# Score range from sums and absolute differences of key pairs, with key differences formed ahead of the loop

## The chip, the cores and the metric

The kernel runs on one core of one Trainium2 chip. A core has TensorE (PE; its weight loads are shown apart as PEld), VectorE (DVE), ScalarE (ACT), GpSimd (POOL) and SyncE (SP), which here only issues transfers. The metric is the device time of one execution in microseconds (us). Before the change the median of three runs is 1267.35 us (1264.89 to 1267.72).

## The reference, cut to what matters

32 samples of 153 rows (25 image rows, 128 text rows), 192 channels. Embedding, then attention with 12 heads of 16 channels in emulated integer arithmetic, then a layer of three experts. The change touches one step of attention, the range of all scores:

```python
attn = jnp.einsum('bhnd,bhmd->bhnm', q, k) * attn_scale
attn, a_scale = fq_act(attn)          # needs attn.min() and attn.max() over everything
attn = log_int_softmax(attn, a_scale) # needs the maximum of each row
```

`fq_act` takes its scale from the smallest and the largest score of all samples, heads and rows. So nothing of the softmax can begin until all scores have been formed once. The kernel forms them twice: once for the range and the row maxima (`range_scores`), and again in `attention`.

## The kernel before, in words

The program is a row of stages, each a block that ends for all engines together: `embed`, `quant_inputs`, `range_h`, `quant_qkv`, `range_scores`, `attention`, `project`, `ffn_inputs`, `experts`. Quantized queries and keys lie in `qk` (bf16) with four heads in the four partition groups of 32, three such tiles of queries and three of keys for each sample.

`range_scores` loops over the 32 samples ("batches", B), two by two, so that each engine has two buffers (`u` is 0 or 1). For one batch there are RT = 15 rows of score tiles: 12 heads with the 128 text queries, and 3 tiles in which the image queries of four heads are stacked. Each tile is 128 x 153.

To keep the heads of one tile apart, a head's keys (or image queries) are copied into a buffer that is zero in the other partition groups: `kb` for keys, `qb` for image queries. The class `Stage` holds this. `load` (lines 677 to 683), on SyncE, issues four transfers for `kb`, one for each partition group, and four more for `qb` if `placing` is false. If `placing` is true, as in `range_scores`, GpSimd writes `qb` with four copies (`place`, line 685). `attention` uses the same class with `placing` false. `free` (line 672) lets a load begin when TensorE has finished the batch two before it. The helper `wait_apart` (line 320) is a wait and, as an instruction of its own, a step of a semaphore `passed`.

Around it, in `range_scores` (line 712 on): TensorE makes five banks of three tiles (L708), each as soon as ScalarE has emptied the same bank of the last batch. ScalarE copies each bank to `score_copy` (L769); before the first bank of a batch it waits until VectorE is done with the copy two before. VectorE takes each row's maximum into `rmax` (L808) and, in a second pass over the same 2295 elements, the smallest value of all (L809). After the loop come small chained steps on VectorE (L814 to L855) for the range and its constants, one reduction over partitions on GpSimd, and on ScalarE, after its last bank, copies into `vbd` (L777) and `pick` (L779). SyncE, after its last load, fills `kb` and `qb` for the first two batches of `attention` when TensorE is done with them.

At the stage's start GpSimd clears `qb` and half of `kb` (L740, L741) and VectorE the other half (L798); SyncE's first transfer waits for all three.

Of the kernel before, what the change touches and what calls it, by code (L numbers as in the profile page):

```python
# [16 lines left out]
P = 128  # L17
# [30 lines left out]
def ds(start, size):  # L48
    return bass.ds(start, size)
# [21 lines left out]
def embed(k, m):  # L71
# [6 lines left out]
    with ExitStack() as st:  # L78
# [17 lines left out]
        img_acc, img_out, conv_ok = k.sem("img_acc"), k.sem("img_out"), k.sem("conv_ok")  # L96
        feat_set, feat_sq, feat_ok, featT_ps, featT_sb, emb_acc = (k.sem(x) for x in ("feat_set", "feat_sq", "feat_ok", "featT_ps", "featT_sb", "emb_acc"))
        power_set, stats1, aggr1, var1_ok, rstd1_ok, scaled_ok, h_ok = (
            k.sem(x) for x in ("power_set", "stats1", "aggr1", "var1_ok", "rstd1_ok", "scaled_ok", "h_ok"))
# [9 lines left out]
        with nc.Block() as block:  # L109
# [14 lines left out]
            @block.gpsimd  # L124
            def _(pool):
                pool.wait_ge(in_ids, 16)

                def gather(g):
                    for b in range(4 * g, 4 * g + 4):
                        pool.indirect_dma_start(out=raw[:, b, :], out_offset=None, in_=d["turns"],  # L130
                                                in_offset=bass.IndirectOffsetOnAxis(ap=ids[:, b:b + 1], axis=0)
                                                ).then_inc(gathered[g % 4], 16)

                def root1(g):
                    pool.wait_ge(aggr1, 4 * g + 4)
# [12 lines left out]
                pool.wait_ge(power_set, 1)  # L148
# [100 lines left out]
            def _(v):  # L249
                v.memset(feat[:, :, :], 0.0).then_inc(feat_set, 1)  # L250
                v.wait_ge(feat_set, 1)
                v.memset(feat[:, :, 0:8], 1.0).then_inc(feat_set, 1)
                v.memset(power[:, :, :], -0.5).then_inc(power_set, 1)
                v.memset(m["vt"][:, :, :], 0.0)
                v.memset(m["vi"][:, :, :], 0.0)
                v.wait_ge(feat_set, 2)

                def features(g):
                    rows = slice(4 * g, 4 * g + 4)
# [41 lines left out]

                features(0)
                v.wait_ge(in_conv, 32)
                v.tensor_tensor(convb[:, :], convb[:, :], posimg[:, :], ALU.add).then_inc(conv_ok, 1)
                v.wait_ge(conv_ok, 1)
                for g in range(G):
                    if g + 1 < G:
                        features(g + 1)
# [352 lines left out]
class Stage:  # L661

    def __init__(self, k, m, name, placing):

        self.m, self.placing = m, placing
        self.kb, self.qb = m["kb"], m["qb"]
        self.loaded = [k.sem(f"{name}_loaded{i}") for i in range(2)]
        self.placed, self.scored = k.sem(name + "_placed"), k.sem(name + "_scored")  # L670
# [41 lines left out]
def range_scores(k, m):  # L712


    NB = RT // 3
    with ExitStack() as st:
        sb = lambda n, s, t=F32: k.sb(n, s, t, st)
        s = Stage(k, m, "rs", True)
        low, copy, spent = sb("score_low", [P, B]), sb("score_copy", [P, 2, RT, N]), sb("score_spent", [P, 2, RT * N], BF16)
        rmax, con, ident, pick = m["rmax"], m["con"], m["ident"], m["pick"]  # L720
        mm1, mm2, own = sb("sm1", [P, 2]), sb("sm2", [P, 2]), sb("pick_own", [P, RT])
        banks = k.ps("rs_banks", [P, NB, 512], F32, st)
        cleared, kept, topped, lowered, sr, sred, vbd_zero = (
            k.sem(x) for x in ("rs_cleared", "rs_kept", "rs_topped", "rs_lowered", "rs_r", "rs_red", "vbd_zero"))
        vbd, own_ok = m["vbd"], k.sem("pick_own_ok")

        def pairs(eng, body):
# [9 lines left out]
        with k.nc.Block() as block:  # L737
            @block.gpsimd
            def _(pool):
                pool.memset(m["qb"][:, :, :, :, :], 0.0).then_inc(cleared, 1)  # L740
                pool.memset(m["kb"][:, 1, :, :, :], 0.0).then_inc(cleared, 1)  # L741
                pool.wait_ge(cleared, 3)
                pairs(pool, lambda n, u: s.place(pool, n, u))
                pool.wait_ge(sr, 1)
                pool.partition_all_reduce(mm2[:, :], mm1[:, :], P, RMAX).then_inc(sred, 1)

            @block.sync
            def _(sp):
                sp.wait_ge(cleared, 3)
                s.load(sp, 0, 0)  # L750
                s.load(sp, 1, 1)
                with sp.Fori(1, B // 2) as i:
                    for u in range(2):
                        s.load(sp, i * 2 + u, u)

                for u in range(2):
                    sp.wait_ge(s.scored, (B - 1 + u) * NB)
                    m["at_stage"].load(sp, u, u)

            @block.scalar  # L760
            def _(act):
                def body(n, u):
                    for b in range(NB):
                        act.wait_ge(s.scored, n * NB + b + 1)
                        if b == 0 and not early(n, 2):

                            act.wait_ge(topped, n - 1)
                            act.wait_ge(lowered, n - 1)
                        act.activation(copy[:, u, 3 * b:3 * b + 3, :].rearrange("p w n -> p (w n)"), banks[:, b, 0:3 * N], ACT.Copy).then_inc(kept, 1)  # L769
                pairs(act, body)  # L770

                act.wait_ge(vbd_zero, 1)
# [7 lines left out]

            @block.tensor
            def _(pe):
                def body(n, half, u):
                    s.ready(pe, n, half, u)
                    for b in range(NB):
                        if not early(n, 1):
                            pe.wait_ge(kept, (n - 1) * NB + b + 1)
                        s.scores_at(pe, n, u, b, banks[:, b, :])
# [7 lines left out]
            def _(v):  # L796
# [7 lines left out]
                with v.Fori(0, B // 2) as i:  # L804
                    for u in range(2):
                        n = i * 2 + u
                        v.wait_ge(kept, n * NB + NB)
                        v.tensor_reduce(rmax[:, n, :], copy[:, u, :, :], AX, ALU.max).then_inc(topped, 1)  # L808
                        v.tensor_scalar(spent[:, u, :], copy[:, u, :, :].rearrange("p t n -> p (t n)"), 1.0, BIG, ALU.mult, ALU.min,  # L809
                                        accum_out=low[:, ds(n, 1)]).then_inc(lowered, 1)  # L810
                v.wait_ge(topped, B)
                v.wait_ge(lowered, B)
                flat = lambda x: x[:, :, :].rearrange("p b t -> p (b t)")
                link(v.tensor_reduce(mm1[:, 0:1], flat(rmax), AX, ALU.max))  # L814
                link(v.tensor_reduce(mm1[:, 1:2], low[:, :], AX, ALU.min, negate=True))
# [4 lines left out]
                v.tensor_scalar(mm1[:, :], mm1[:, :], con[:, 0:1], None, ALU.mult).then_inc(sr, 1)  # L820
                v.wait_ge(sred, 1)
                quant_params(v, link, mm2, qa)
                inv = qa[:, 1:2]
# [20 lines left out]
                link(v.tensor_scalar(flat(rmax), flat(rmax), c(0), None, ALU.mult))  # L844
# [862 lines left out]
def build(nc, d):  # L1707
    with ExitStack() as stack:
# [25 lines left out]
        with att:  # L1734
# [8 lines left out]
            m["at_stage"] = Stage(k, m, "at", False)  # L1743
            range_scores(k, m)
            attention(k, m)
            project(k, m)
# [69 lines left out]
```

## Time and profile before

| what | value |
|---|---|
| median of three runs | 1267.35 us |
| the profiled execution's own time | 1267.97 us |
| its span, first to last instruction | 1266.2 us |
| mean granted TensorE clock | 0.73 |
| VectorE busy | 1081.3 us, 85% |
| ScalarE busy | 716.5 us, 57% |
| TensorE busy | 701.3 us, 55% |
| GpSimd busy | 92.1 us, 7% |
| key blocks loaded by SyncE (both stages) | 256 transfers of 28.7 KB |

Busy time is the time in which an engine works on an instruction; issuing transfers, register and semaphore instructions are not counted in it. "Idle before, releaser" is the time for which an engine stood still ahead of an instruction, and what ended it. SPq is SyncE's queue: the start and the length of the instruction that issues a transfer, not of the transfer. "To landing" is the time from an issue to the transfer's completion. The clock is a share of TensorE's full 2.4 GHz; 0.50 is its other level, 1.2 GHz. Matmul records overlap, so a group's mean length is longer than the distance between two.

### The profile page before, as it was taken

Reading aid. Unit: us, or ns where it says so; the run is one execution under the profiler, and the core shown is the slowest. Engines: PE = TensorE matmul, PEld = TensorE weight load, DVE = VectorE, ACT = ScalarE, POOL = GpSimd, SP = SyncE. Lnnn points to the kernel's source line nnn. Section 1 sums busy time; section 2 is a strip of 40 time slices with the busy share of each in tenths; the row PEclk is TensorE's granted clock in tenths of the full one; section 3 lists DMA queues with packets and bytes.
Section 4 is the critical chain, followed back from the end, with each engine's and each line's share of the span. In section 5 each row is a group of like instructions: output and inputs, shape, how many; then the busy total and the mean of one; then the engine's idle time right before and its main releaser. Section 6 shows DMA issues by size and latency. Waiting matters only on the chain. (4 is left out here: it accounts for less than half of the span.)

```text
span 1266.2 us, 22220 instructions
## 1 busy us (share of the span) xinstructions
PE 701.3 (55%) x5608; PEld 486.4 (38%) x5609; DVE 1081.3 (85%) x2534; ACT 716.5 (57%) x1271; POOL 92.1 (7%) x203
## 2 busy tenths in 40 slices
PE   4850165744544346657665666656423031299997
PEld 3640144433322123334333333334212021288987
DVE  5768898879999979999999999999999657566676
ACT  0451000955445559999999999999921221144543
POOL 5830000012121000000000000000000000000000
PEclk9875576975555576787878877877757555599999
DMA  4001000001111110101001000010000300245543
GB/s 147 3 1 62 0 0 0 1 7 30 24 23 25 20 34 20 24 22 22 20 19 24 22 21 19 22 23 17 10 1 1 140 0 0 102 147 195 189 175 110
DMA packets 84216, 54.48 MB, mean 43 GB/s; under 512 B 53688, under 2 KB 83160, under 8 KB 83928
## 3 DMA queue, kind: packets, MB, share of 16 engines
q1 hardware_dynamic: 83160, 53.97, 13.9%
q0 software_dynamic: 1024, 0.13, 0.2%
q8 instruction: 14, 0.23, 0.1%
q14 instruction: 18, 0.15, 0.0%
HBM read 11.77 MB, written 3.76 MB: 12 GB/s over the span
## 5 line engine op out<-in xcount | busy, mean ns | idle before, releaser
L1166 DVE SCALAR_TENSOR_TENSOR expo<-expo,con,pow 128x153 f32<-128x153 f32 x480 | 146.1, 375 | 0.7 <-ACT expo L1118 0.7
L769 ACT ACTIVATE score_copy<-rs_banks 128x459 f32<-128x459 f32 x160 | 74.7, 564 | 92.5 <-DVE score_spent L809 74.8
L1013 PE MATMUL at_pT<-identb,vi 128*128 128x128 bf16 x480 | 61.1, 292 | 90.4 <-ACT vi L1092 89.9
L1118 ACT ACTIVATE expo<-at_rem,con 128x459 f32<-128x459 f32 x160 | 97.0, 642 | 15.8 <-PE at_rem L998 8.3
L708 PE MATMUL rs_banks<-kb,qk 128*128 128x153 bf16 x384 | 57.7, 329 | 84.7 <-ACT score_copy L769 72.3
L997 PE MATMUL at_rem<-below,identb 128*128 128x459 bf16 x160 | 69.1, 432 | 60.3 <-ACT expo L1118 58.9
L603 ACT ACTIVATE qi<-pq,biasp,ap 128x306 int16<-128x306 f32 x96 | 48.0, 727 | 94.0 <-PE pq L566 94.0
L1215 DVE CUSTOM_DVE_ANT_0 weight_top<-weight_top,line 128x2448 uint16<-128x2448 uint16 x64 | 83.8, 1351 | 8.5 <-ACT line L1109 5.7
L1081 ACT ACTIVATE octave<-at_banks,con 128x459 int16<-128x459 f32 x160 | 90.2, 650 | 0.8 <-PE at_banks L708 0.2
L703 PE MATMUL at_banks<-pick,row_top 128*128 128x459 bf16 x160 | 78.2, 489 | 17.7 <-ACT octave L1081 17.1
L808 DVE TENSOR_REDUCE rmax<-score_copy 128x2295 f32 x32 | 81.3, 2542 | 4.1 <-ACT score_copy L769 4.1
L1191 DVE TENSOR_TENSOR expo<-expo,inv_total 128x1224 f32<-128x1224 f32 x64 | 83.6, 1347 | 0.0
L1013 PEld LDWEIGHTS at_pT<-identb,vi 128*128 128x128 bf16 x480 | 42.3, 129 | 104.6 <-issue 76.4
L809 DVE TENSOR_SCALAR_CACHE_REDUCE score_spent<-score_copy 128x2295 bf16<-128x2295 f32 x32 | 81.2, 2536 | 0.0
L1610 PE MATMUL e_p<-X,e_ws 128*128 (+1 forms) x960 | 72.2, 235 | 13.4 <-DMA e_ws<-w1l 13.2
L1109 ACT ACTIVATE line<-expo,p_index 128x1224 f32<-128x1224 f32 x64 | 76.6, 1251 | 2.0 <-DVE expo L1191 2.0
L708 PEld LDWEIGHTS rs_banks<-kb,qk 128*128 (+1 forms) x384 | 35.8, 126 | 104.2 <-issue 81.0
L1649 ACT ACTIVATE e_g<-e_p,b1s 128x153 f32<-128x153 f32 x192 | 58.9, 392 | 29.4 <-PE e_p L1610 28.2
L1072 ACT ACTIVATE pT_text<-at_pT,p_index 128x768 int16<-128x768 int16 (+1 forms) x96 | 71.6, 779 | 6.4 <-PE at_pT L1013 4.5
L1610 PEld LDWEIGHTS e_p<-X,e_ws 128*128 128x128 bf16 x960 | 65.9, 100 | 18.8 <-issue 15.1
L1092 ACT ACTIVATE vi<-weight_top,p_index 128x1024 int16<-128x1024 int16 x64 | 71.5, 1117 | 0.0
L998 PE MATMUL at_rem<-octave,octave_step 128*128 128x459 bf16 x160 | 68.2, 426 | 0.0
(348 smaller groups left out, 1880.6 us busy)
## 6 DMA issues: line engine op xcount, KB each, us to landing
e_ws<-w1h SPq DMA_DIRECT2D x32, 384.0 KB, 2.9
e_ws<-w1l SPq DMA_DIRECT2D x32, 384.0 KB, 3.2
kb<-qk SPq DMA_DIRECT2D x256, 28.7 KB, 2.0
patches<-in_patches SPq DMA_DIRECT2D x4, 768.0 KB
vi<-vt SPq DMA_DIRECT2D x32, 96.0 KB, 2.0
out<-e_ot SPq DMA_DIRECT2D x32, 96.0 KB, 1.9
f_w<-in_w SPq DMA_DIRECT2D x1, 2304.0 KB, 8.5
qb<-qk SPq DMA_DIRECT2D x128, 6.0 KB, 1.8
```

The lines of the kernel that those rows point to most:

```text
L703: pe.matmul(bank[:, 0:3 * N], top, pick[:, 3 * i:3 * i + 3, :].rearrange("p w n -> p (w n)"), start=True, stop=False, skip_group_check=True)
L708: mm = pe.matmul(bank[:, w * N:(w + 1) * N], lhs, rhs, start=(top is None), stop=True, skip_group_check=(top is not None))
L808: v.tensor_reduce(rmax[:, n, :], copy[:, u, :, :], AX, ALU.max).then_inc(topped, 1)
L809: v.tensor_scalar(spent[:, u, :], copy[:, u, :, :].rearrange("p t n -> p (t n)"), 1.0, BIG, ALU.mult, ALU.min, accum_out=low[:, ds(n, 1)]) ...
L1013: mm = pe.transpose(pT[:, slot, j * P:(j + 1) * P], src, identb[:, :])
L1081: act.activation(bank(dist, b), banks[:, b % 3, 0:3 * N], ACT.Relu, scale=c(0)).then_inc(evicted, 1)
L1109: act.activation(flat(line, half), flat(ex, half), ACT.Identity, scale=0.5, bias=index[:, 2:3]).then_inc(y_done, 1)
L1118: act.activation(bank(ex, b), rem[:, (u + b) % 2, 0:3 * N], ACT.Square, bias=c(5)).then_inc(sq_done, 1)
L1166: ins = v.scalar_tensor_tensor(ex[:, t, :], ex[:, t, :], c(7), pw[:, t, :].bitcast(BF16), ALU.add, ALU.mult, accum_out=tot[:, t:t + 1])
L1191: v.tensor_tensor(ex[:, half, :], ex[:, half, :], share, ALU.mult).then_inc(w_done, 1)
L1215: v.tensor_tensor(flat(top, half).bitcast(I32), flat(top, half).bitcast(I32), flat(line, half).bitcast(I32), ALU.add).then_inc(i_done, 1)
L1610: mm = pe.matmul(o, ws[:, kk, w, kt, fs], X[:, plane, ds(n * N, N)], start=(a == 0), stop=(a == len(parts) - 1))
```

## The change

For two scores a and b of one row, the larger is (a + b + |a - b|) / 2 and the smaller (a + b - |a - b|) / 2. A row of 153 keys is paired: key c with key c + 76, for c from 0 to 76 (W = 77 pairs; key 76 is in two of them). TensorE now forms for each tile the sum over a pair, by two accumulating products of 77 columns, and the difference, by one product with the difference of the keys. ScalarE copies the sums to `both` and takes the absolute value of the differences into `gap`. VectorE adds the two to `high` and reduces that to the row maxima, and in one fused instruction (`tensor_tensor_reduce`) takes `gap - both` and its largest value, which is carried from batch to batch in two columns of `low`. The factor 0.5 goes into later instructions. A batch is now 3 groups of 5 rows, each with a bank of sums and a bank of differences: six banks, six evictions of 385 columns.

The key differences `kd` are formed by GpSimd, one subtraction for each batch, ahead of the loop's use (`gap_done` counts them). SyncE spreads them into `kdb`, zero in the other partition groups, with four transfers for each batch. `Stage` is called with `placing` false in this stage, so `load` issues eight transfers, and GpSimd's copies into `qb` go. A fourth clearing, of `kdb`, is added on GpSimd. `Stage` has the count of TensorE's steps per batch as a parameter. In `embed`, two semaphores are merged into `feat_set`.

```diff
 # Stage
-            eng.wait_ge(self.scored, (n - 1) * (RT // 3))
+            eng.wait_ge(self.scored, (n - 1) * self.per_row)
 # range_scores
-    NB = RT // 3
+    W, PER = N // 2 + 1, 5
+    NB = RT // PER
+    PARTS_ROW = 2 * NB
-        s = Stage(k, m, "rs", True)
+        s = Stage(k, m, "rs", False, PARTS_ROW)
+        kd, kdb = sb("key_gap", [P, B, HT, W], BF16), sb("key_gap_heads", [P, 2, HT, 4, W], BF16)
 # GpSimd
-                pool.wait_ge(cleared, 3)
-                pairs(pool, lambda n, u: s.place(pool, n, u))
+                pool.memset(kdb[:, :, :, :, :], 0.0).then_inc(cleared, 1)
+                pool.wait_ge(cleared, 4)
+                with pool.Fori(0, B) as n:
+                    pool.tensor_tensor(kd[:, n, :, :], m["qk"][:, n, HT:2 * HT, 0:W], m["qk"][:, n, HT:2 * HT, N - W:N], ALU.subtract).then_inc(gap_done, 1)
 # SyncE
-                s.load(sp, 0, 0)
-                s.load(sp, 1, 1)
-                with sp.Fori(1, B // 2) as i:
-                    for u in range(2):
-                        s.load(sp, i * 2 + u, u)
+                def load(n, u):
+                    s.load(sp, n, u)
+                    wait_apart(sp, gap_done, n + 1, k.passed)
+                    for j in range(4):
+                        r = slice(32 * j, 32 * j + 32)
+                        sp.dma_start(kdb[r, u, :, j, :], kd[r, n, :, :]).then_inc(gap_in[u], 16)
+                pairs(sp, load)
 # ScalarE
-                            act.wait_ge(topped, n - 1)
-                            act.wait_ge(lowered, n - 1)
-                        act.activation(copy[:, u, 3 * b:3 * b + 3, :]..., banks[:, b, 0:3 * N], ACT.Copy).then_inc(kept, 1)
+                        for x, (dst, func) in enumerate(((both, ACT.Copy), (gap, ACT.Abs))):
+                            act.wait_ge(s.scored, n * PARTS_ROW + 2 * b + x + 1)
+                            if b == 0 and x == 0 and not early(n, 2):
+                                act.wait_ge(raised, n - 1)
+                                act.wait_ge(lowered, n)
+                            act.activation(dst[:, u, PER * b:PER * b + PER, :]..., banks[:, x, b, 0:PER * W], func).then_inc(kept, 1)
 # TensorE, for each of the 15 rows, first x = 0, then x = 1
+                    if x == 1:
+                        return pe.matmul(out, lhs, gaps, start=True, stop=True)
+                    pe.matmul(out, lhs, keys(0), start=True, stop=False)
+                    return pe.matmul(out, lhs, keys(N - W), start=False, stop=True)
 # VectorE
-                        v.tensor_reduce(rmax[:, n, :], copy[:, u, :, :], AX, ALU.max).then_inc(topped, 1)
-                        v.tensor_scalar(spent[:, u, :], copy[:, u, :, :]..., 1.0, BIG, ALU.mult, ALU.min,
-                                        accum_out=low[:, ds(n, 1)]).then_inc(lowered, 1)
+                    v.wait_ge(kept, n * PARTS_ROW + PARTS_ROW)
+                    if not early(n, 1):
+                        v.wait_ge(topped, n)
+                    v.tensor_tensor(high, both[:, u, :, :], gap[:, u, :, :], ALU.add).then_inc(raised, 1)
+                    wait_apart(v, lowered, n + 1, k.passed)
+                    v.tensor_tensor_reduce(spent[:, u, :, :], gap[:, u, :, :], both[:, u, :, :], 1.0, low[:, u:u + 1], ALU.subtract, ALU.max,
+                                           accum_out=low[:, 1 - u:2 - u]).then_inc(lowered, 1)
+                    v.wait_ge(raised, n + 1)
+                    v.tensor_reduce(rmax[:, ds(n, 1), :]..., high, AX, ALU.max).then_inc(topped, 1)
```

## Rows read from the trace of the kernel before

**Rows 1.** The page, busy us, share of the span and instructions of each engine.
```profile
PE 701.3 (55%) x5608; PEld 486.4 (38%) x5609; DVE 1081.3 (85%) x2534; ACT 716.5 (57%) x1271; POOL 92.1 (7%) x203
```
**Rows 2.** Windows: PE, PEld, DVE, ACT, POOL busy us; clock, DMA share, GB/s.
```profile
286.11:443.47 157.36, 71.39 (x463) 43.85 (x461) 157.35 (x96) 79.60 (x170) 30.87 (x118) 0.50 0.12 24
```
**Rows 3.** Groups on VectorE, same window: busy us, mean ns, idle before.
```profile
L808 DVE TENSOR_REDUCE rmax<-score_copy 128x2295 f32 x32 | 81.3, 2542 | 4.1 <-ACT score_copy L769 4.1
L809 DVE TENSOR_SCALAR_CACHE_REDUCE score_spent<-score_copy 128x2295 bf16<-128x2295 f32 x32 | 81.2, 2536 | 0.0
```
**Rows 4.** Waits in the same window: us in total, times, longest.
```profile
ACT score_copy L769 <- DVE score_spent L809: 74.8, 29, 2.6
```
**Rows 5.** Timeline from 340 us: start us, length us, instruction.
```profile
340.17 2.54 DVE L808 TENSOR_REDUCE rmax<-score_copy 128x2295 f32 x1
...
345.08 2.54 DVE L808 TENSOR_REDUCE rmax<-score_copy 128x2295 f32 x1
...
345.98 1.81 PE L708 MATMUL rs_banks<-kb,qk 128*128 128x153 bf16 x12 [2.59 <-ACT score_copy L769]
```
**Rows 6.** Transfers: KB and us to landing; source line L681, ns min/median/max.
```profile
kb<-qk SPq DMA_DIRECT2D x256, 28.7 KB, 2.0
qb<-qk SPq DMA_DIRECT2D x128, 6.0 KB, 1.8
...
L681 SPq DMA_DIRECT2D kb<-qk x256: 607/607/1480, 278.9 to 869.7; - x128
```
**Rows 7.** Timeline of SyncE's queue behind the loop, code without a loop.
```profile
427.65 0.61 SPq L683 DMA_DIRECT2D qb<-qk  x1
428.30 0.61 SPq L681 DMA_DIRECT2D kb<-qk  x1
```
**Rows 8.** Timeline of SyncE's queue in the loop, one batch.
```profile
343.53 2.83 SPq L681 DMA_DIRECT2D kb<-qk  x4
```
**Rows 9.** Waits of SyncE's queue from 300 to 430 us.
```profile
SPq L681 <- PE rs_banks L708: 45.0, 26, 1.9
```
**Rows 10.** Timeline at the loop's end, VectorE and ScalarE.
```profile
443.38 0.09 DVE L809 DVE_READ_ACCUMULATOR score_spent<-score_copy  x1
443.57 0.65 DVE L814 TENSOR_REDUCE sm<-rmax 128x1 f32<-128x480 f32 x1
...
454.28 0.15 DVE L855 TENSOR_SCALAR con<-con 128x1 f32<-128x1 f32 x1
...
435.93 8.48 ACT L777 ACTIVATE vbd<-vi 32x384 bf16<-32x384 bf16 x16
```
**Rows 11.** Groups on VectorE elsewhere: busy us, mean ns, idle before.
```profile
L1191 DVE TENSOR_TENSOR expo<-expo,inv_total 128x1224 f32<-128x1224 f32 x64 | 83.6, 1347 | 0.0
...
L296 DVE SCALAR_TENSOR_TENSOR Hres<-Hres,rstd,beta 128x192 f32<-128x192 f32 x32 | 11.2, 410 | 0.0
...
L293 DVE SCALAR_TENSOR_TENSOR Hres<-pemb,mv,gamma 128x192 f32<-128x192 f32 x32 | 11.0, 407 | 7.7 <-POOL rstd L138 7.7
...
L1360 DVE CUSTOM_DVE_ANT_1 pj_Y<-pj_py,pj_row 128x384 f32<-128x384 f32 x20 | 9.9, 554 | 0.4 <-PE pj_py L1297 0.3
```
**Rows 12.** Timeline of SyncE's queue in attention's loop, one load.
```profile
565.76 0.53 SPq L941 DMA_DIRECT2D v_image_row<-vbd  x1
566.85 0.70 SPq L681 DMA_DIRECT2D kb<-qk  x1
...
572.18 0.61 SPq L683 DMA_DIRECT2D qb<-qk  x1
```
**Rows 13.** Timeline of TensorE, six transposes at the lower clock.
```profile
555.37 0.82 PE L1013 MATMUL at_pT<-identb,vi 128*128 128x128 bf16 x6 [2.55 <-ACT vi L1092]
```
**Rows 14.** Timeline at the stage's start.
```profile
277.23 1.63 POOL L741 MEMSET kb<- 128x1836 bf16 x1
278.89 21.42 SPq L681 DMA_DIRECT2D kb<-qk  x25
```
**Rows 15.** Source line L1577, ns min/median/max.
```profile
L1577 SPq DMA_DIRECT2D out<-e_ot x32: 332/354/383, 1112.0 to 1262.3; - x32
```

More of the change, by code:

```diff
@@ L252, in _ @@
                 v.memset(feat[:, :, 0:8], 1.0).then_inc(feat_set, 1)
[L253 removed]
+                v.memset(power[:, :, :], -0.5).then_inc(feat_set, 1)
                 v.memset(m["vt"][:, :, :], 0.0)
                 v.memset(m["vi"][:, :, :], 0.0)
[L256 removed]
+                v.wait_ge(feat_set, 3)
                 def features(g):
@@ L303, in _ @@
                 v.wait_ge(in_conv, 32)
-                v.tensor_tensor(convb[:, :], convb[:, :], posimg[:, :], ALU.add).then_inc(conv_ok, 1)
-                v.wait_ge(conv_ok, 1)
+                v.tensor_tensor(convb[:, :], convb[:, :], posimg[:, :], ALU.add).then_inc(feat_set, 1)
+                v.wait_ge(feat_set, 4)
                 for g in range(G):
@@ L712, in range_scores @@
 def range_scores(k, m):
-    NB = RT // 3
+    W, PER = N // 2 + 1, 5
+    NB = RT // PER
+    PARTS_ROW = 2 * NB
     with ExitStack() as st:
         sb = lambda n, s, t=F32: k.sb(n, s, t, st)
-        s = Stage(k, m, "rs", True)
-        low, copy, spent = sb("score_low", [P, B]), sb("score_copy", [P, 2, RT, N]), sb("score_spent", [P, 2, RT * N], BF16)
+        s = Stage(k, m, "rs", False, PARTS_ROW)
+        low, spent = sb("score_low", [P, 2]), sb("score_spent", [P, 2, RT, W], BF16)
+        both, gap = (sb("score_" + x, [P, 2, RT, W]) for x in ("both", "gap"))
+        high = m["line"][:, :, :].rearrange("p t n -> p (t n)")[:, 0:RT * W].rearrange("p (t n) -> p t n", n=W)
+        kd, kdb = sb("key_gap", [P, B, HT, W], BF16), sb("key_gap_heads", [P, 2, HT, 4, W], BF16)
         rmax, con, ident, pick = m["rmax"], m["con"], m["ident"], m["pick"]
         mm1, mm2, own = sb("sm1", [P, 2]), sb("sm2", [P, 2]), sb("pick_own", [P, RT])
-        banks = k.ps("rs_banks", [P, NB, 512], F32, st)
-        cleared, kept, topped, lowered, sr, sred, vbd_zero = (
-            k.sem(x) for x in ("rs_cleared", "rs_kept", "rs_topped", "rs_lowered", "rs_r", "rs_red", "vbd_zero"))
+        banks = k.ps("rs_banks", [P, 2, NB, 512], F32, st)
+        cleared, kept, raised, topped, lowered, sr, sred, vbd_zero, gap_done = (
+            k.sem(x) for x in ("rs_cleared", "rs_kept", "rs_raised", "rs_topped", "rs_lowered", "rs_r", "rs_red", "vbd_zero", "rs_gap_done"))
+        gap_in = [k.sem(f"rs_gap_in{u}") for u in range(2)]
         vbd, own_ok = m["vbd"], k.sem("pick_own_ok")
@@ L763, in body @@
                     for b in range(NB):
-                        act.wait_ge(s.scored, n * NB + b + 1)
-                        if b == 0 and not early(n, 2):
-                            act.wait_ge(topped, n - 1)
-                            act.wait_ge(lowered, n - 1)
-                        act.activation(copy[:, u, 3 * b:3 * b + 3, :].rearrange("p w n -> p (w n)"), banks[:, b, 0:3 * N], ACT.Copy).then_inc(kept, 1)
+                        for x, (dst, func) in enumerate(((both, ACT.Copy), (gap, ACT.Abs))):
[3 more added lines that the diff above has]
+                                act.wait_ge(lowered, n)
+                            act.activation(dst[:, u, PER * b:PER * b + PER, :].rearrange("p w n -> p (w n)"), banks[:, x, b, 0:PER * W], func).then_inc(kept, 1)
                 pairs(act, body)
@@ L782, in _, with product @@
             def _(pe):
+                qk = m["qk"]
+                def product(n, u, i, x):
+                    b, w = divmod(i, PER)
+                    out = banks[:, x, b, w * W:(w + 1) * W]
+                    t, j = divmod(i, 4)
+                    if t < HT:
+                        lhs, keys, gaps = qk[:, n, t, 0:NT], lambda c: s.kb[:, u, t, j, c:c + W], kdb[:, u, t, j, :]
+                    else:
+                        t = i - H
+                        lhs, keys, gaps = s.qb[:, u, t, :, :].rearrange("p j n -> p (j n)"), lambda c: qk[:, n, HT + t, c:c + W], kd[:, n, t, :]
+                    if x == 1:
+                        return pe.matmul(out, lhs, gaps, start=True, stop=True)
+                    pe.matmul(out, lhs, keys(0), start=True, stop=False)
+                    return pe.matmul(out, lhs, keys(N - W), start=False, stop=True)
                 def body(n, half, u):
                     s.ready(pe, n, half, u)
+                    pe.wait_ge(gap_in[u], half * 64 + 64)
                     for b in range(NB):
-                        if not early(n, 1):
-                            pe.wait_ge(kept, (n - 1) * NB + b + 1)
-                        s.scores_at(pe, n, u, b, banks[:, b, :])
+                        for x in range(2):
+                            if not early(n, 1):
+                                pe.wait_ge(kept, (n - 1) * PARTS_ROW + 2 * b + x + 1)
+                            for w in range(PER):
+                                mm = product(n, u, PER * b + w, x)
+                            mm.then_inc(s.scored, 1)
                 for u in range(2):
@@ L803, in _, with extremes @@
                 v.tensor_tensor(own[:, :], own[:, :], ident[:, 2 * RT:3 * RT], ALU.add).then_inc(own_ok, 1)
[L804 to L807, printed above, removed]
-                        v.tensor_reduce(rmax[:, n, :], copy[:, u, :, :], AX, ALU.max).then_inc(topped, 1)
-                        v.tensor_scalar(spent[:, u, :], copy[:, u, :, :].rearrange("p t n -> p (t n)"), 1.0, BIG, ALU.mult, ALU.min,
-                                        accum_out=low[:, ds(n, 1)]).then_inc(lowered, 1)
+                v.memset(low[:, :], -BIG).then_inc(lowered, 1)
+                def extremes(n, u):
+                    v.wait_ge(kept, n * PARTS_ROW + PARTS_ROW)
+                    if not early(n, 1):
+                        v.wait_ge(topped, n)
[4 more added lines that the diff above has]
+                    v.wait_ge(raised, n + 1)
+                    v.tensor_reduce(rmax[:, ds(n, 1), :].rearrange("p o t -> p (o t)"), high, AX, ALU.max).then_inc(topped, 1)
+                pairs(v, extremes)
                 v.wait_ge(topped, B)
-                v.wait_ge(lowered, B)
+                v.wait_ge(lowered, B + 1)
                 flat = lambda x: x[:, :, :].rearrange("p b t -> p (b t)")
                 link(v.tensor_reduce(mm1[:, 0:1], flat(rmax), AX, ALU.max))
-                link(v.tensor_reduce(mm1[:, 1:2], low[:, :], AX, ALU.min, negate=True))
+                link(v.tensor_reduce(mm1[:, 1:2], low[:, :], AX, ALU.max))
                 qh, qa = m["qh"], m["qa"]
```

26 lines of the change are left out of this document (14 added, 12 removed).

## The prediction

> **What bounds the kernel now.** The page's first line says that VectorE is busy for 85% of the span [rows 1], but that is a mean over stages, so I went on to the stage that the change touches, the loop of `range_scores`. In the table by windows, from the first reduction's start to the last one's end (157.36 us), VectorE is busy all the time, ScalarE half of it, TensorE less than half at a granted clock of 0.50, its 1.2 GHz level [rows 2]. The groups of that window show what VectorE does: 32 reductions of 2542 ns and 32 cache-reduces of 2536 ns, with no idle time but the 4.1 us before the first [rows 3]. The waits say the same from the other side: ScalarE waited 74.8 us for `score_spent` [rows 4], and the others stand behind ScalarE. The timeline of one batch gives the period: a reduction starts at 340.17 and the next at 345.08, so 4.91 us for a batch, two passes 2.45 us apart [rows 5].
>
> So VectorE sets the pace, and it is what the change relieves. The next question is who has room for what the change hands over. Look at SyncE's queue, whose work is in no busy share. Each of 256 transfers of a key block keeps it for 607 ns [rows 6], and each of an image-query block for 0.61 us too [rows 7], though that is 6.0 KB against 28.7 KB [rows 6]: the issue goes by the transfer, not by its bytes. In this loop four issues take 2.83 us from the first start to the last end, so they start (2.83 - 0.61)/3 = 0.74 us apart [rows 8]; then SyncE waits for TensorE, 45.0 us of 130 [rows 9]. Four transfers cost it 4 x 0.74 = 2.96 of 4.91 us: nothing is free there for three times as many.
>
> **The change part by part.**
>
> VectorE. Two passes over 15 x 153 = 2295 elements go, three over 15 x 77 = 1155 come. Unchained passes start 2.455 us apart now; in proportion to the elements that is 1.24 us for 1155, and a fixed part does not shrink, so I take 1.27 from start to start. One alone is 2.54 long now, 1.28 in proportion, and I take 1.35. The add waits for the reduction directly in front of it (`high` has one copy), so that one counts in full with some 0.10 us for the wait, as between 443.38 + 0.09 and 443.57 [rows 10]. The fused subtract and maximum is not in the trace. Nearest are a product of two f32 arrays (1224 elements, 1347 ns) and the custom operation with an accumulator at L1360 (384 elements, 554 ns) [rows 11]: 1.10 ns an element in the one, like the reductions, and 1.44 in the other, where the fixed part weighs more. At 1.44 the fused step would be 1.66, 0.4 above my 1.27; I stay with 1.27, by the row nearest in size. Sum: 1.27 + 1.27 + 1.45 = 3.99 us a batch against 4.91, 29 us over 32 batches if VectorE still set the pace.
>
> The Trainium skill has a rule against this operation (Vector Engine (DVE) Microarchitecture Reference, "Points that are easy to get wrong"): a two-source operation of the scalar_tensor_tensor shape whose SBUF sources are both not bf16 runs at half throughput. Here the rows speak against it: 192 elements with both sources f32 in SBUF (L296) take 410 ns, and with one of them in PSUM (L293) 407 ns [rows 11]. By the Trainium skill the fused step would take 1.2 us more, a batch 5.2 us of VectorE; by the rows it takes 4.0. For my sum this is 1.2 us, once, at the tail.
>
> SyncE. Before, `load` issued four transfers a batch, and GpSimd wrote the image queries with four copies. Now `placing` is false, so `load` issues eight, and the loop adds four for the key gaps: twelve. `kdb<-kd` has the shape of `kb<-qk` (32 partitions, one contiguous source run, three rows to write), so I price it by that row. What is 12 in a loop? In straight-line code issues start 0.65 us apart (427.65, 428.30) [rows 7], in this loop 0.74 [rows 8], and in attention's loop, which issues the same eight, (572.18 - 566.85)/7 = 0.76 [rows 12]. I take this loop's: 12 x 0.74 = 8.88 us. To this come two waits on computed values (`free`, and the one for `gap_done` with its semaphore step). Attention's queue, at a wait of this kind that has long been met, takes 0.56 us from the end of one issue (565.76 + 0.53) to the next (566.85) instead of 0.13, so 0.43 more [rows 12]; the second wait lies between 0 and that, and I take 0.2. A batch of SyncE is then 9.5 us, between 9.1 and 9.8 with 0.74, and 8.1 if the straight-line spacing held.
>
> Which wait ends last, then? The next load needs TensorE to have finished two batches back. TensorE starts 2.0 us after the last issue (landing [rows 6]) and needs 4.8 us (6.8 at most), so it is done 7 to 9 us after that load, while SyncE works for 9.5 on the one between. SyncE never waits: it is a chain of issues and nothing else. VectorE's 3.99 us, its new own waits and all of ScalarE's six evictions of 385 columns (79.6 us busy over some 32 batches of five [rows 2], so at most 79.6/32 x 6/5 = 3.0 us) lie inside 9.5. VectorE's saving is paid to nobody.
>
> TensorE. 45 products of 77 columns stand for 15 of 153, each with its own weight load. Not in the trace is a 77-column product with 128-column weights. Below, 77/1.2 = 64 ns each, 2.9 us; above, the spacing of 153 columns, 12 in 1.81 us, so 0.15 each, 6.8 us [rows 5]. Six transposes of 128 columns with 128-column weights take 0.82 us with the tail of the last one, which leaves room for 128/1.2 = 107 ns each [rows 13]; I take that, since the weight load may be the longer part: 4.8 us. It stands on the path once, for the last batch.
>
> GpSimd. 128 copies go, 32 subtractions of 231 elements come. The trace has no such operation there; between nothing and the 1.63 us of a pass over 1836 elements [rows 14], batch n is ready at 1.63 n us at the latest, and its transfers go out at 9.5 n. Hidden. Its new memset of 1848 elements is not: SyncE started at 278.89, behind the third clearing (277.23 + 1.63) [rows 14], and waits for a fourth now, 1.64 us.
>
> The merged semaphores in `embed` order the same memsets (40 elements beside 2048) and cost nothing I can price above 0.1 us. Factors of 0.5 ride in instructions that are there anyway.
>
> **The sum.** SyncE starts at 278.89 + 1.64 = 280.5. Two straight-line loads: 24 x 0.65 plus 0.4 for the first waits, to 296.5. Thirty loads in the loop: 30 x 9.5 = 285, to 581.5. Its last issue began 0.6 earlier and lands 2.0 later, 582.9. TensorE 4.8, to 587.7; ScalarE's last eviction 0.5; VectorE add, fused step and reduction 4.0: 592.2. The loop ended at 443.47 before [rows 10], so +148.7. Behind it, VectorE's chain of small steps from 443.57 to 454.4 stays [rows 10], and covers ScalarE's sixteen copies into `vbd` (8.5 us [rows 10], begun when its evictions are over, 4 us ahead of the loop's end, with `pick` behind them) and the transfers for attention, whose last eight start when TensorE is done and need 8 x 0.65 = 5.2 us. The profiled execution took 1267.97 us (span 1266.2); 1267.97 + 148.7 = 1416.7. The runs' median is 0.6 below it: **1416 us**.
>
> The Trainium skill says of transfers from several engines that they save only the issuing sequencer's time, "which is usually small relative to the DMA itself" (DMA: Bandwidth & Descriptors, "Issuing engines are not separate DMA queues"). By it the twelve issues would not count beside the work, and the sum would be the first rival's. The row shows 0.607 us of issue beside 2.0 us of landing, and landings overlap where issues don't.
>
> **Rivals.**
> 1. The issues hide, and VectorE stays the bound: -29 us, and +9 for a first batch whose twelve issues, four more microseconds of TensorE and a fourth clearing come before VectorE's start. 1248 us. It needs 3.99/12 = 0.33 us an issue; break-even is 4.91/12 = 0.41. For it: the output transfers of L1577 issue in 354 ns [rows 15]. Against it: 256 records of exactly this shape, 607 as lowest and median [rows 6]. Chance 0.04.
> 2. The same, with the fused step at half rate: 5.2 us a batch, 32 x 0.3 = +9 and +9: 1286 us. Chance 0.03.
> 3. SyncE sets the pace, with straight-line spacing: 12 x 0.65 + 0.3 = 8.1, 30 x 1.4 = 42 less: 1375 us. Against: both loops shown have 0.74 or more. Chance 0.08.
> 4. TensorE becomes the bound because a short product costs more than a long one: at twice today's 1.81/12 = 0.15 us [rows 5], 45 take 13.6 us, 32 x (13.6 - 4.9) = +278: near 1546. It decides from 7.5 us a batch, 0.17 a product. Against: nothing in a product of half the columns is longer. Chance 0.02.
> Forecast: 0.83.
>
> **Range and chances.** Within the forecast, 9.1 gives 1404; 0.80 for a transfer, were three kinds of address dearer than attention's mixture at 0.76, with 0.6 of waits gives 10.2 and 1437. I widen to the third rival's side in part: 1385 to 1440. Under 0.2% nothing can be told from no change here. Faster 0.04 (rival 1), same 0.01, slower 0.95.
>
> **What would show it.** Right: SyncE's issues run without a gap from 280 to about 581, twelve in 9.5 us; TensorE's long wait is for `kdb<-kd` or its peers; VectorE waits for ScalarE's `gap` about 5 us in each batch; the stage is about 306 us long, the clock 0.50 in it; attention, its trace shifted, keeps its length. Wrong: an issue of `kdb` well under 600 ns, a wait of SyncE for TensorE in the loop, or VectorE without idle time there.

## The result

The changed kernel takes 1418.93 us (median of four runs, 1417.2 to 1419.12) against 1266.76 (four runs, 1264.89 to 1267.72): 1.120 times as long, 95% interval 1.118 to 1.122. Forecast was 1416. The profiled execution took 1417.2 us, with a span of 1415.4.

The page after the change: busy time of each engine over the span, and three of its rows by slices.

```profile
PE 724.0 (51%) x6568; PEld 532.3 (38%) x6569; DVE 1052.1 (74%) x2567; ACT 724.8 (51%) x1303; POOL 82.1 (6%) x108
...
DVE  5769897833444334579999999999999965846666
ACT  0440008522222222579999999999993122034553
...
PEclk9965579855555555578897877878865655579999
```

Beside [rows 1], VectorE has 29 us less work and the kernel is 149 us longer in span. VectorE's row shows the hole: eight slices at 3 or 4 tenths, 283 us. The same hole is in ScalarE's row, and no engine of the page fills it. Work that no row of busy time shows must set the pace. The stage by windows, and its waits from 300 to 570 us:

```profile
290.00:590.00 300.00, 98.88 (x1440) 93.40 (x1440) 126.51 (x126) 85.80 (x197) 19.50 (x27) 0.56 0.12 22
```

```profile
ACT score_both L784 <- PE rs_banks L813: 193.8, 29, 8.5
PEld rs_banks L812 <- issue: 184.3, 28, 8.2
PE rs_banks L812 <- DMA key_gap_heads<-key_gap: 179.4, 28, 8.1
DVE line L846 <- ACT score_gap L784: 157.6, 29, 6.8
```

Read it as a chain, from VectorE back: it waits for ScalarE, ScalarE for TensorE, TensorE for the last transfers of a load. The DMA engines are busy for 0.12 of the time, as they were before [rows 2], so they are not what is full. The same view for SyncE's own queue has no row in this window; before, it waited 45.0 us of 130 [rows 9]. Its timeline shows one batch:

```profile
564.07 0.63 SPq L683 DMA_DIRECT2D kb<-qk  x1
564.83 0.61 SPq L685 DMA_DIRECT2D qb<-qk  x1
565.57 0.61 SPq L683 DMA_DIRECT2D kb<-qk  x1
...
569.30 0.61 SPq L685 DMA_DIRECT2D qb<-qk  x1
570.29 2.84 SPq L767 DMA_DIRECT2D key_gap_heads<-key_gap  x4
573.37 0.63 SPq L683 DMA_DIRECT2D kb<-qk  x1
```

Twelve issues, one behind the other, then the next load at once. From 403.81 to 573.37, 18 loads later, it is 9.42 us a load; VectorE's period was 4.91 [rows 5]. The stage's end, on VectorE, which answers to [rows 10], and the groups on VectorE from 300 to 560 us, which answer to [rows 3]:

```profile
587.65 1.36 DVE L846 TENSOR_TENSOR line<-score_both,score_gap 128x1155 f32<-128x1155 f32 x1 [5.28 <-ACT score_gap L784]
588.93 1.42 DVE L848 CUSTOM_DVE_ANT_0 score_spent<-score_gap,score_both,score_low 128x1155 bf16<-128x1155 f32 x1
590.27 0.08 DVE L848 DVE_READ_ACCUMULATOR2_ANT score_low<- 128x1 f32 x1
590.27 1.35 DVE L851 TENSOR_REDUCE rmax<-line 128x1155 f32 x1
```

```profile
L848 DVE CUSTOM_DVE_ANT_0 score_spent<-score_gap,score_both,score_low 128x1155 bf16<-128x1155 f32 x27 | 38.6, 1429 | 0.0
L846 DVE TENSOR_TENSOR line<-score_both,score_gap 128x1155 f32<-128x1155 f32 x28 | 38.2, 1365 | 152.4 <-ACT score_gap L784 152.4
```

The three passes are as short as the change wants them, and VectorE stands still for 152.4 us of 260 ahead of them. The loop ends at 591.62 against 443.47 [rows 10], 148.2 later. From there little differs: from the first transpose of `attention` to the first reduction of `project` it is 474.7 us before (455.0 to 929.7) and 473.9 after (603.1 to 1077.0), and from there to the end of the span 336.5 before and 338.4 after.

### The profile page after: what moved, and what is told of

It is laid out like the page before. It is cut to its first block and busy times, and to the rows that moved or that the text cites. A ratio compares the mean times of both kernels' runs of the same rounds, so it can differ in the third digit from the quotient of the medians.

```text
span 1415.4 us, 24977 instructions
## 1 busy us (share of the span) xinstructions
PE 724.0 (51%) x6568; PEld 532.3 (38%) x6569; DVE 1052.1 (74%) x2567; ACT 724.8 (51%) x1303; POOL 82.1 (6%) x108
## 5 line engine op out<-in xcount | busy, mean ns | idle before, releaser
L846 DVE TENSOR_TENSOR line<-score_both,score_gap 128x1155 f32<-128x1155 f32 x32 | 44.0, 1374 | 183.1 <-ACT score_gap L784 183.1
L812 PE MATMUL rs_banks<-kb,qk 128*128 128x77 bf16 x384 | 62.1, 263 | 216.6 <-DMA key_gap_heads<-key_gap 211.8
L784 ACT ACTIVATE score_both<-rs_banks 128x385 f32<-128x385 f32 x96 | 47.3, 493 | 236.9 <-PE rs_banks L813 232.0
L812 PEld LDWEIGHTS rs_banks<-kb,qk 128*128 (+1 forms) x384 | 48.7, 140 | 222.3 <-issue 222.3
L710 PE MATMUL at_banks<-kb,qk 128*128 128x153 bf16 x384 | 64.7, 294 | 0.0
## 6 DMA issues: line engine op xcount, KB each, us to landing
kb<-qk SPq DMA_DIRECT2D x256, 28.7 KB, 1.9
```

What stands on the lines that cost most here:

```text
L812: pe.matmul(out, lhs, keys(0), start=True, stop=False)
```

## The experiments

All are compared with the kernel before, run on the same chip; its median was 1265 to 1267 us each time. Three questions: is it the number of issues, and not bytes, rows or landing; whose time does an issue take; and what is the new arithmetic worth when nothing else is in the way? The diffs are cut to the lines that matter. Not shown in them: where `placing` is true, the clearing of `vbd` is counted on `own_ok` instead of a semaphore of its own, outside the loop.

**Eight transfers, not twelve (`e1_place`).** The base of this and of all others is the changed kernel, except for `e10_before8`.

```diff
-        s = Stage(k, m, "rs", False, PARTS_ROW)
+        s = Stage(k, m, "rs", True, PARTS_ROW)
# GpSimd, for each batch: the key difference, then the four copies into qb
+                    pool.tensor_tensor(kd[:, n, :, :], ..., ALU.subtract).then_inc(gap_done, 1)
+                    for j in range(4):
+                        ins = pool.tensor_copy(s.qb[r, u, :, j, :], m["qk"][r, n, 0:HT, IW:N])
```

> The changed kernel, but GpSimd writes the image queries again (with `placing` true), so SyncE issues 8 transfers a batch, not 12. If SyncE's issues are the chain: a batch is 8 x 0.74 + 0.5 = 6.4 us against the 9.42 measured, 30 x 3.0 = 89 less in the loop and 8 x 0.65 = 5 less ahead of it: 1325 us. If the path is instead one of latency (TensorE waits for the last transfer to land, whatever is issued before it), the four fewer issues do not matter: 1405 to 1419 us.

Measured: 1325.88 us (1.048, 1.046 to 1.050). The sum with 0.74 an issue holds to 1 us, and SyncE's queue still has no wait from 290 to 460 us. The theory of latency falls: the last transfer is the same one, and four fewer ahead of it took 93 us away.

**The same with the kernel before as base (`e10_before8`).** The old arithmetic, with SyncE loading the image queries too.

```diff
-        s = Stage(k, m, "rs", True)
+        s = Stage(k, m, "rs", False)
-                pairs(pool, lambda n, u: s.place(pool, n, u))
```

> The kernel before, with one edit: `placing` false, so SyncE loads the image queries too, 8 transfers a batch instead of 4, and GpSimd writes nothing. Everything else as before. If SyncE's issues become the chain: 8 x 0.74 + 0.45 = 6.4 us a batch against VectorE's 4.91, 30 x 1.5 = 45 more, and 2.6 for the first batch's four extra issues: 1313 us. If the transfers hide beside VectorE (their landing is 2 us, their bytes few): 1265 to 1270 us.

Measured: 1311.79 us (1.036, 1.033 to 1.038). This single flag makes the old kernel 45 us slower. Its timeline on VectorE shows the pace passing to SyncE, with 6.0 us between two reductions here where it was 4.91 [rows 5], and 6.3 on the mean (18 of them from 300.72 to 414.67 us); SyncE's queue has no wait in the loop:

```profile
351.96 2.54 DVE L807 TENSOR_REDUCE rmax<-score_copy 128x2295 f32 x1 [1.54 <-ACT score_copy L768]
354.42 2.54 DVE L808 TENSOR_SCALAR_CACHE_REDUCE score_spent<-score_copy 128x2295 bf16<-128x2295 f32 x1
...
357.97 2.54 DVE L807 TENSOR_REDUCE rmax<-score_copy 128x2295 f32 x1 [1.00 <-ACT score_copy L768]
```

**Fewer bytes (`e3_quarter`).**

```diff
-                        sp.dma_start(kdb[r, u, :, j, :], kd[r, n, :, :]).then_inc(gap_in[u], 16)
+                        sp.dma_start(kdb[r, u, :, j, 0:19], kd[r, n, :, 0:19]).then_inc(gap_in[u], 16)
```

> The changed kernel, with the key-gap transfers cut to the first 19 of 77 columns (the rest of the gap buffers stays zero, so the differences of those pairs are left out); as many transfers and rows as before. If an issue costs by the transfer: no change, 1417 to 1421 us. If bytes bound the loop: 10.8 of 49 KB less per four transfers, some 20% of the loop, 60 us less: 1360 us.

Measured: 1417.09 us, within 2 us of the changed kernel. The transfers carry 3.6 KB, not 14.4, and their issue is 607 ns all the same:

```profile
key_gap_heads<-key_gap SPq DMA_DIRECT2D x128, 3.6 KB, 1.8
```

```profile
L767 SPq DMA_DIRECT2D key_gap_heads<-key_gap x128: 607/607/627, 286.9 to 580.6; - x128
```

**More rows in fewer transfers (`e4_joined`).**

```diff
+                    if u == 1:
+                        wait_apart(sp, gap_done, n + 1, k.passed)
+                        for j in range(4):
+                            sp.dma_start(kdb[r, :, :, j, :], kd[r, ds(n - 1, 2), :, :]).then_inc(gap_in[0], 16)
# TensorE, both batches of a pair
-                    pe.wait_ge(gap_in[u], half * 64 + 64)
+                    pe.wait_ge(gap_in[0], half * 64 + 64)
```

> The changed kernel, with the key gaps of two batches in one transfer (twice the rows, half the transfers: 10 a batch on the mean). If an issue costs by the transfer, a batch is 10 x 0.74 + 0.4 = 7.9 us: 30 x 1.5 = 46 less, 1373 us. If it costs by the row that it describes (192 instead of 96), a joined issue takes 1.2 us and nothing is won: 1410 to 1419 us.

Measured: 1434.8 us, 16 slower than the changed kernel, so the time I gave by either theory is wrong. The price is not. The issue of twice the rows, and SyncE's one wait from 300 to 570 us:

```profile
L768 SPq DMA_DIRECT2D key_gap_heads<-key_gap x64: 607/607/617, 291.2 to 595.1; - x64
```

```profile
SPq L683 <- PE rs_banks L812: 57.0, 13, 4.4
```

A joined issue costs what a single one does. What I had left out is the order: now neither batch of a pair can start before the pair's last transfer, TensorE does both at once, and the next load of a buffer waits for it, 4.4 us a pair. The round of load, landing and TensorE, which twelve issues had covered, is open. The sum with this wait comes out: 20 issues of 0.74, twice 0.4 for the waits on computed values and 4.4 make 20.0 us a pair, and from 339.83 to 359.91 the queue takes 20.1.

**Issues from another engine (`e7_act`).** SyncE four, ScalarE's queue four.

```diff
+                def spread(n, u):
+                    wait_apart(act, gap_done, n + 1, k.passed)
+                    for j in range(4):
+                        act.dma_start(kdb[r, u, :, j, :], kd[r, n, :, :]).then_inc(gap_in[u], 16)
# ScalarE, in batch n behind the first pair of banks
+                        if b == 0 and more:
+                            spread(n + 1, 1 - u)
```

> GpSimd writes the image queries, and ScalarE's queue issues the four key-gap transfers of a batch, one batch ahead; SyncE is back to four. If an issue occupies the engine that makes it as it does SyncE, ScalarE takes 6 x 0.49 + 4 x 0.74 + 0.4 = 6.3 us a batch and sets the pace: 1325 us, as with eight transfers on SyncE. If issues from a second queue are as good as free, the batch falls to VectorE's 4.05 us or the load's round of (4 issues + landing + TensorE)/2 = 4.3 us: 1250 to 1258 us.

Measured: 1301.56 us (1.027, 1.025 to 1.030), nearer to the first theory than to the second. ScalarE's timeline shows the four issues between two evictions:

```profile
350.51 0.49 ACT L796 ACTIVATE score_gap<-rs_banks 128x385 f32<-128x385 f32 x1
350.56 2.78 ACTq L786 DMA_DIRECT2D key_gap_heads<-key_gap  x4
353.45 0.49 ACT L796 ACTIVATE score_both<-rs_banks 128x385 f32<-128x385 f32 x1 [2.45 <-issue]
353.84 0.49 ACT L796 ACTIVATE score_gap<-rs_banks 128x385 f32<-128x385 f32 x1
```

An issue takes ScalarE's time as it takes SyncE's (614 ns the median here). My 6.3 us was too much because evictions overlap: they start 0.39 us apart, so six take 2.3 and not 2.9. VectorE's adds start 5.74 and 5.39 us apart in this trace.

**No spreading by transfers: copies on GpSimd (`e2_pool`).**

```diff
-                        sp.dma_start(kdb[r, u, :, j, :], kd[r, n, :, :]).then_inc(gap_in[u], 16)
+                        ins = pool.tensor_copy(kdb[r, u, :, j, :], kd[r, n, :, :])
```

> GpSimd writes both the image queries and the spread key gaps, by eight copies a batch; SyncE is back to 4 transfers. If SyncE was all that stood in the way, the next bound shows: VectorE with 4.05 us a batch (1250 us, 17 less than before the change), or GpSimd with 0.73 + 4 x 0.26 + 4 x 0.5 + waits = 4.4 us a batch (1262 us). The theory that the sums and differences themselves cost more than two passes (three passes, an own wait on each) says at least 4.9 a batch: 1275 or more.

Measured: 1308.81 us (1.035, 1.033 to 1.036). GpSimd is the bound, as one of my cases had it, but with 6.0 us a batch (20 batches in 120 us) and not 4.4. Its timeline, two batches:

```profile
352.58 1.63 POOL L765 COPY key_gap_heads<-key_gap 32x231 bf16 x4
354.60 1.25 POOL L756 TENSOR_TENSOR key_gap<-qk  x1 [0.39 <-POOL key_gap_heads L765]
356.29 1.82 POOL L762 COPY qb<-qk 32x96 bf16 x4 [0.43 <-PE rs_banks L821]
358.14 3.80 POOL L765 COPY key_gap_heads<-key_gap 32x231 bf16 x4
```

The same four copies take 1.63 us at 352.6, while VectorE stands still (350.6 to 354.0), and 3.80 us from 358.1 on, while it adds (358.46) and runs its fused pass (359.74). VectorE loses too: the fused pass takes 1628 ns on the mean against 1429.

**No spreading at all: negated queries (`e8_negated`).** The difference of a pair is q with the first key plus -q with the second, accumulated in PSUM. It needs no buffer of spread gaps.

```diff
+                        pe.matmul(out, lhs, keys(0), start=True, stop=False)
+                        return pe.matmul(out, neg[:, u, t, :], keys(N - W), start=False, stop=True)
# ScalarE, one batch ahead
+                    act.activation(neg[:, u, :, :], m["qk"][:, n, 0:HT, 0:NT], ACT.Copy, scale=-1.0).then_inc(gap_in[0], 1)
```

> No spread key gaps at all: for the text queries the difference is the product with the first keys plus the product of the negated queries with the second ones (12 more products a batch); ScalarE negates the queries, one activation a batch, one batch ahead; GpSimd writes the image queries and forms the differences for the image rows. SyncE has 4 transfers. If VectorE's three short passes are worth what the changed kernel's trace shows (1.28 + 1.35 + 1.40 us), a batch is 4.05 us, or 4.3 to 4.5 if the round of issue (3.4), landing (1.9) and TensorE (57 x 0.065 = 3.7) divided by two ends last: 1245 to 1255 us, 1% below the kernel before. If sums and differences do not pay even then, 1265 or more.

Measured: 1251.1 us (0.987, 0.985 to 0.990). VectorE is the bound again, with a batch of 4.26 us (4.23 on the mean), and the kernel is 1.3% faster than before the change. The fourth clearing is gone here too, with the buffer that it cleared. Two things keep it from 4.05: the add takes 1521 ns on the mean beside GpSimd's reads, and its own wait. And the stage starts late:

```profile
276.31 1.63 POOL L749 MEMSET kb<- 128x1836 bf16 x1
285.35 0.57 POOL L755 TENSOR_TENSOR key_gap<-qk 128x231 bf16<-128x231 bf16 x1 [7.41 <-issue]
```

**No subtraction on GpSimd (`e11_scalar`).** The image rows' differences come from negated keys.

```diff
+                    act.activation(negk[:, u, :, :], m["qk"][:, n, HT:2 * HT, N - W:N], ACT.Copy, scale=-1.0).then_inc(gap_in[0], 1)
# GpSimd
-                    pool.tensor_tensor(kd[:, n, :, :], ..., ALU.subtract).then_inc(gap_done, 1)
+                pairs(pool, lambda n, u: s.place(pool, n, u))
```

> As e8_negated, but the image rows' differences come from negated keys as well: ScalarE negates 231 key columns a batch beside the queries (0.4 us more of its time), TensorE has three products more, and GpSimd forms no differences; it only writes the image queries. In e8_negated the first subtraction began 7.4 us after GpSimd's last clearing with nothing to wait for, and TensorE stood for it. If that pause belongs to the subtraction, VectorE's loop begins some 5 to 7 us earlier, and GpSimd reads less beside VectorE's adds: 1239 to 1246 us. If it belongs to any first work behind the clearings, or ScalarE's added 0.4 us or TensorE's products now end last: 1250 or more.

Measured: 1241.58 us (0.981, 0.979 to 0.982). GpSimd's first copy begins right behind the clearing:

```profile
277.40 1.63 POOL L749 MEMSET kb<- 128x1836 bf16 x1
279.10 2.39 POOL L691 COPY qb<-qk 32x96 bf16<-32x96 bf16 x8
```

So the pause belongs to the subtraction. What it consists of isn't in the trace. It is only half of the 9.5 us gained: VectorE's first add comes 11.1 us after the stage's start instead of 16.2, and a batch takes 4.10 us on the mean instead of 4.23, 4.4 us in all.

**Two buffers for `high` (`e12_twohigh`).**

```diff
-        high = m["line"]...
+        high2 = sb("score_high", [P, 2, RT, W])
-                        v.wait_ge(topped, n)
+                        v.wait_ge(topped, n - 1)
```

> e11_scalar with two buffers for `high`, so VectorE's add no longer waits for the reduction directly in front of it. The traces show 1.45 us from that reduction's start to the next add against 1.28 between passes that do not wait. If this own wait costs what the difference says, 32 x 0.15 = 5 us less than e11_scalar; if GpSimd's copies or the load's round end last instead, no difference (within 2 us).

Measured: 1234.7 us (0.975, 0.974 to 0.977), 6.9 below `e11_scalar` where 5 were expected. The timeline of one batch: an add starts 1.27 us behind the reduction, not 1.45.

```profile
351.15 1.34 DVE L862 TENSOR_REDUCE rmax<-score_high 128x1155 f32 x1
352.42 1.43 DVE L857 TENSOR_TENSOR score_high<-score_both,score_gap 128x1155 f32<-128x1155 f32 x1
353.78 1.42 DVE L859 CUSTOM_DVE_ANT_0 score_spent<-score_gap,score_both,score_low 128x1155 bf16<-128x1155 f32 x1
355.13 0.08 DVE L859 DVE_READ_ACCUMULATOR2_ANT score_low<- 128x1 f32 x1
355.13 1.35 DVE L862 TENSOR_REDUCE rmax<-score_high 128x1155 f32 x1
```

A batch is 3.98 us (351.15 to 355.13; 3.93 on the mean of all), and this version is 31 us faster than the kernel before, and 184 faster than the changed one.

## Why the prediction was right

The forecast was 1416, measured 1418.9, and the mechanism is the one that was forecast. By its steps:

1. *SyncE becomes a chain of issues.* Shown by its queue without a wait in the loop, and by the dose: 12, 8 and 4 transfers a batch. Twelve give 9.42 us a batch; eight on either arithmetic give the times worked out with 0.74 an issue, 0.9 us above the one and 1.2 below the other.
2. *12 x 0.74 + 0.6 = 9.5 us a batch.* 9.42 measured in the steady loop. The thirty loads from 298.05 to 582.32 took 284.3 us, 0.7 less than the 285 of the sum and not 2.4, since two early issues took 1.81 and 1.21 us instead of 0.61 (at 300.28 and 322.26). The traces don't say why.
3. *The first rival.* The sentence of the Trainium skill beside it (DMA: Bandwidth & Descriptors, "Issuing engines are not separate DMA queues") calls the time of an issue usually small beside the transfer. Issue is 0.607 us against 1.9 of landing, but landings overlap and issues of one queue don't. Here the measurement decides against it, from SyncE and from ScalarE, for 3.6 KB as for 28.7.
4. *VectorE's passes: 1.27 + 1.27 + 1.45.* In the chain of the changed kernel they cost once, and 4.0 us. When they set the pace, with one copy of `high` as priced, they were 4.09 us (`e11_scalar`: 1.28, 1.36 and 1.45); the 3.98 are with two buffers, where the third term no longer has a wait. The half rate of the Trainium skill's rule (Vector Engine (DVE) Microarchitecture Reference, "Points that are easy to get wrong") would have made the fused pass some 2.5 us; it is 1.43 us with both sources f32 in SBUF. The trace records the pass as a custom operation, though, and no run shows whether it is of the rule's shape; the row that is of that shape by its name is L296 [rows 11].
5. *TensorE's 4.8 us for the last batch.* Too much. Its products of 77 columns start 0.065 us apart at 1.2 GHz (291.48, 291.54, 291.61), so the columns set the spacing and the weight load hides: 45 take 2.9 us. This is the term that was most out. In the sum: the first product of the last batch at 583.93, the last eviction's end at 587.62, 3.7 against 5.3, 1.6 less.
6. *The start.* The stage began 1.6 us earlier than in the execution before, which no edit accounts for: the stage starts between 274.2 and 277.0 us in the traces of all versions, so this part of the agreement is luck. The fourth clearing cost its 1.64. GpSimd's first subtraction, priced as hidden, was not: it began 7.8 us behind the clearings, and the first transfer of a gap waited for it, at 287.28 where the eighth issue had ended at 284.18. 3.1 us, a term that the sum lacked: it had batch n ready "at 1.63 n us at the latest", which has no start-up in it.
7. *The signs.* The clock in the stage was 0.56 and not 0.50, and changed no term of weight. The 306 us hold only from the same start as before (286.11) to the new end: by VectorE's own first and last pass the loop is 297 us long, since its first add comes at 294.96. SyncE's one gap behind its first issue is that of step 6.

The trace of step 6, GpSimd's subtraction and the transfer that waited for it:

```profile
283.57 0.61 SPq L685 DMA_DIRECT2D qb<-qk  x1
286.61 0.57 POOL L754 TENSOR_TENSOR key_gap<-qk  x1 [7.80 <-issue]
287.28 2.56 SPq L767 DMA_DIRECT2D key_gap_heads<-key_gap  x4
```

In the order of the sum, measured against forecast: start -1.7 us, the two first loads +3.2, thirty loads -0.7, the last landing +0.2, TensorE and the last eviction -1.6. The loop ended at 591.62 instead of 592.2, and the stages behind it took 1.1 us more than before, for which the sum had nothing. Small errors of both signs, then, which cancel in part by chance: 1416.7 for the profiled execution, 1417.2 measured.

Rival 1's 1248 us for a kernel bound by VectorE is near what `e8_negated` measures (1251.1), in part by chance: that run has a longer batch than the rival's 3.99, and no fourth clearing. The rival's +9 is also a slip; the parts that it names, 8 x 0.65, 4 and 1.64, make 10.8. But the arithmetic itself was never the fault: the same sums and differences are in the fastest version here, 1234.7 us.

## What to carry to other kernels

Count transfers for the engine that issues them as you count instructions for one that computes: here 0.61 us each, 0.74 in a loop, whether they carry 3.6 KB or 28.9, and the view of busy time does not show it. The price is that of this kind of transfer: the output transfers of L1577 cost 0.35 [rows 15], and no run shows what makes the difference. Before adding transfers to a loop, compare their number by that price with the loop's period, not their bytes with the bandwidth. Before joining transfers, ask what the joined one does to the order in which buffers come free: here it cost more than the saved issues gave. Doing without the buffer (a negated operand and one more accumulating product) was worth more here than any way of filling it.

## What the runs showed of the hardware that was not expected

GpSimd's reads and VectorE's two-source passes slow each other. A copy of 32 x 96 elements takes 263 ns on the mean beside single-source passes (the kernel before), and 642 to 713 ns in `e12_twohigh` and `e8_negated`, where VectorE adds and runs fused passes; the add takes 1521 ns on the mean in `e8_negated` against 1365. The groups on GpSimd, of the kernel before (all of it), of `e8_negated` (290 to 410 us) and of `e12_twohigh` (300 to 400 us):

```profile
L689 POOL COPY qb<-qk 32x96 bf16 (+1 forms) x128 | 33.7, 263 | 110.9 <-PE rs_banks L708 106.7
```

```profile
L761 POOL COPY qb<-qk 32x96 bf16 x112 | 79.9, 713 | 13.7 <-PE rs_banks L828 6.7 <-PE rs_banks L832 2.1 <-PE rs_banks L830 1.1
```

```profile
L691 POOL COPY qb<-qk 32x96 bf16 x104 | 66.8, 642 | 34.2 <-PE rs_banks L821 30.8
```

These means hide two kinds of copy. In `e12_twohigh` the shortest takes 257 ns, the median 264, the longest 1470, about as long as a whole two-source pass. One batch of `e8_negated` shows which is which:

```profile
355.33 1.53 DVE L866 TENSOR_TENSOR line<-score_both,score_gap 128x1155 f32<-128x1155 f32 x1
355.98 1.00 POOL L761 COPY qb<-qk 32x96 bf16 x1 [0.33 <-PE rs_banks L828]
356.78 1.42 DVE L868 CUSTOM_DVE_ANT_0 score_spent<-score_gap,score_both,score_low 128x1155 bf16<-128x1155 f32 x1
358.13 1.35 DVE L871 TENSOR_REDUCE rmax<-line 128x1155 f32 x1
358.37 0.57 POOL L761 COPY qb<-qk 32x96 bf16 x2
```

The first copy ends about when the add does, the second, from 357.02, about when the fused pass does, and the two beside the reduction take 0.57 us together.

It is what a rule says in the Trainium skill (SBUF — State Buffer, "Who interferes with whom"): a VectorE instruction with two SBUF inputs contends with a GpSimd instruction that reads SBUF, and one with at most one, outside the two-port modes, does not. The trace agrees, for both sides of it.

GpSimd's first subtraction in the stage began 6.8 to 7.8 us after its last clearing in the seven traces that have one, with no wait for any engine; a copy in its place began within 0.1 us. The Trainium skill has a load of some 6 us ahead of the first call of a newly loaded GpSimd kernel (GPSIMD Engine Reference, "2.1 Instruction dispatch"); no run here shows whether that is what passes in the pause.

TensorE's weight load of 128 columns does not hold back products of 77: pairs of load and product start 0.065 us apart at the 1.2 GHz level, which is 77 columns and nothing more. At a granted clock of 1.00 (`e12_twohigh`, 353.13 to 354.00 us) they start 0.038 us apart, where 77 columns would be 0.032, so there something else counts too; no run shows what.
